# Filter spectra of an FFT layer stored with a frequency's 32 channels side by side, through three slots and copies on POOL

## The reference

```
qkv = x @ w_qkv;  q = softmax(q, -1);  k = softmax(k, tokens)      # 4 heads of 32
x = x + layernorm((v^T k applied to q) @ w_out + b_out)
def _stu(u, sigma, phi, Mu, Mpp, Mpm):                              # u: (b, t, d)
    U_plus  = irfft(rfft(phi) * rfft(u))[:, :t]                     # 16 filters
    U_minus = the same on u with alternating signs
    return einsum('btkd,k,kde->bte', U_plus,  sigma**.25, Mpp)
         + einsum('btkd,k,kde->bte', U_minus, sigma**.25, Mpm) + ar(Mu, u)
t = t + sum over 4 fractions of _stu on the first T // frac tokens, weighted by a one-hot choice
```

## Time and profile before

| | |
|---|---|
| median of 3 runs | 379.24 us (376.47 to 379.54) |
| profiled execution: time, span | 377.4 us, 374.0 us |
| mean granted TensorE clock | 0.989 of full speed |
| PE busy | 341.5 us (91%) |
| DVE busy | 228.9 us (61%) |
| ACT busy | 190.7 us (51%) |
| POOL busy | 35.5 us (9%), 38 instructions |

### The profile page before, as it was taken

The page is one execution under the profiler, slowest core; times in us unless marked ns, Lnnn a source line. Parts: engine busy times, 40 slices in busy tenths (PEclk is TensorE's granted clock), DMA queues, the critical chain, the costliest instruction groups (busy, mean ns, idle before and its releaser), DMA issues.

```text
span 374.0 us, 9464 instructions
## 1 busy us (share of the span) xinstructions
PE 341.5 (91%) x4044; PEld 228.4 (61%) x4044; DVE 228.9 (61%) x461; ACT 190.7 (51%) x415; POOL 35.5 (9%) x38
## 2 busy tenths in 40 slices
PE   7969999999998999998889999799998899999890
PEld 2545666566646899956556379257646554773790
DVE  5679768689848403156956764643446476245894
ACT  2988688988868300044862656530346215033460
POOL 4027512122210001000000000000000000000000
PEclk9999999999999999999999999999999899999997
DMA  8960000000070000020000000000000000000004
GB/s 232 127 197 1 2 4 2 2 4 2 3 169 3 4 4 2 4 59 2 0 2 2 0 3 0 4 0 2 2 0 2 0 3 0 2 2 1 0 2 115
DMA packets 7426, 8.95 MB, mean 24 GB/s; under 512 B 3840, under 2 KB 6544, under 8 KB 7056
## 3 DMA queue, kind: packets, MB, share of 16 engines
q1 hardware_dynamic: 5718, 7.28, 9.1%
q10 hardware_dynamic: 1664, 1.05, 0.9%
HBM read 5.70 MB, written 1.05 MB: 18 GB/s over the span
## 4 chain that ended last, share of the span: by engine, by line
PE 64%; DVE 14%; ACT 10%; issue 5%; DMA 4%; SPq 2%; DVEq 0%; ACTq 0%
PE bank L665 30%; PE bank L1098 6%; PE bank L277 5%; PE bank L271 4%; DMA arena<-in_w_spec 4%; PE bank L1025 4%; PE bank L1036 3%; PE bank L865 2%; PE bank L889 2%; ACT lnv L376 2%; SPq L561 1%; ACT rs L381 1%; DVE arena L1796 1%; PE bank L778 1%; PE bank L1155 1%
## 5 line engine op out<-in xcount | busy, mean ns | idle before, releaser
L370 ACT ACTIVATE sq<-bank 128x512 f32<-128x512 f32 x33 | 19.4, 591 | 64.1 <-PE bank L271 50.4
L665 PE MATMUL bank<-xn,sb_w_attn 128*128 128x512 f32 x64 | 34.5, 621 | 3.7 <-ACT attn_scratch L1233 1.9
L665 PE MATMUL bank<-sb_consts 128*128 128x512 f32 (+1 forms) x80 | 35.4, 553 | 0.0
L277 PE MATMUL bank<-sq,sb_consts 128*128 128x512 f32 x66 | 34.7, 611 | 0.5 <-ACT sq L370 0.2
L376 ACT ACTIVATE lnv<-bank 128x512 f32<-128x512 f32 x33 | 19.7, 596 | 30.2 <-PE bank L277 29.9
L1098 PEld LDWEIGHTS bank<-arena,sb_w_late 128*128 128x128 f32 x180 | 23.0, 190 | 10.9 <-DVE arena L1854 8.0
L665 PE MATMUL bank<-arena 64*32 64x256 f32 (+4 forms) x466 | 26.6, 381 | 2.5 <-ACT arena L1266 1.2
L1098 PE MATMUL bank<-arena,sb_w_late 128*128 128x128 f32 (+1 forms) x180 | 26.4, 283 | 1.5 <-DVE arena L1854 0.3
L611 POOL TENSOR_TENSOR attn_scratch<-attn_scratch 128x512 f32<-128x512 f32 x16 | 20.4, 1275 | 72.1 <-DVE attn_scratch L1567 72.1
L1036 PE MATMUL bank<-arena,sb_w_late 128*128 128x128 f32 x136 | 26.3, 277 | 0.0
L1025 PE MATMUL bank<-arena,sb_consts 128*128 128x128 f32 x136 | 26.1, 276 | 0.1
(11 more groups left out here) (208 smaller groups left out, 625.3 us busy)
## 6 DMA issues: line engine op xcount, KB each, us to landing
sb_w_late<-in_w_late SPq DMA_DIRECT2D x1, 1100.5 KB, 18.6
arena<-in_w_spec SPq DMA_DIRECT2D x4, 256.0 KB
arena<-arena SPq DMA_DIRECT2D x4, 256.0 KB, 4.1
arena<-fourier SPq DMA_DIRECT2D x1, 768.0 KB, 16.4
sb_w_attn<-in_w_attn SPq DMA_DIRECT2D x1, 641.0 KB, 8.2
xR<-in_x ACTq DMA_DIRECT2D x4, 128.0 KB, 3.1
xR<-in_x SPq DMA_DIRECT2D x4, 128.0 KB, 4.1
arena<-arena SPq DMA_DIRECT2D x4, 128.0 KB, 2.3
```

The costliest lines, as they stand in the source:

```text
L277: pe.matmul(bank[:, var_bank(i), :], mean32, sq[:, i % 2, :], start=True, stop=True)\
L370: act.activation(sq[:, i % 2, :], bank[:, centre_bank(i), :], ACT.Square).then_inc(S("ln_squared"), 1)
L665: return mm(ps, lhsT, rhs, start=True, stop=True)
```

## The change

FI becomes 1: w lies as (n e) for each part, a frequency's 32 channels side by side, and one channel's frequencies 32 floats (128 bytes) apart. ACT's second and third activation of a turn no longer write to `w_f`, but without gaps to `turned`, three slots (turn m uses m mod 3) that lie in the memory of `toep`. POOL copies a slot to `w_f` in `spread_turn(m)`, two copies a turn, 32 in all, each counting `spectra`. In POOL's stream the copies of a step's turns stand ahead of `q_normalise` of the same unit. New waits: POOL for `filt_sb` of the turn; ACT, from turn 3 on, ahead of its second activation for the copies of turn m - 3; SP ahead of the toep DMAs for all 32 copies; TensorE ahead of the first pass for all 32.

```diff
--- before.py
+++ after.py
@@ -56,7 +56,8 @@
 HT = T // 2
 FREQ = HT
 LAGS = T // 4
-FI = 8
+FI = 1
+TURNS = 3
 TRI_ORDER = [2, 3, 0, 1]
 DFT_BANKS = [6, 7, 0, 1, 2, 5, 3, 7]
 
@@ -171,6 +172,9 @@
         SEG_T = [None, None, T // 4, T // 8]
         SEG_AT = [None, None, 0, T // 4]
         toep = arena[:, AT_TOEP:AT_TOEP + N_TOEP].rearrange("p (t e) -> p t e", e=C)
+
+        turned = arena[:, AT_TOEP:AT_TOEP + 2 * TURNS * 4 * FREQ]\
+            .rearrange("p (w m k n) -> p w m k n", w=2, m=TURNS, k=2)
 
 
 
@@ -576,6 +580,7 @@
 
             sp.wait_ge(S("filt_zero"), 1)
             sp.wait_ge(S("filt_sb"), C // 2)
+            sp.wait_ge(S("spectra"), C)
             for n in (3, 2):
                 for r in range(NQ):
                     sp.dma_start(toep[C * r:C * r + C, SEG_AT[n]:SEG_AT[n] + SEG_T[n], :],
@@ -612,7 +617,17 @@
                 pool.sem_inc(S("q_norm"), 1)
 
 
+            def spread_turn(m):
+                pool.wait_ge(S("filt_sb"), m + 1)
+                for w_ in (1, 0):
+                    to = slice(0, 2 * C if w_ else P)
+                    pool.tensor_copy(w_f[w_][to, m::C // 2, :, :],
+                                     turned[to, w_, m % TURNS, :, :].rearrange("p k (n i) -> p k n i", i=FI))\
+                        .then_inc(S("spectra"), 1)
+
             for u in range(U):
+                for m in filter_turn(u, 0) + filter_turn(u, 1):
+                    spread_turn(m)
                 q_normalise(u)
                 if u == 0:
                     pool.wait_ge(S("sig4"), 1)
@@ -896,6 +911,7 @@
 
             pe.wait_ge(S("x_f_act"), 4)
             pe.wait_ge(S("x_f_dve"), 4)
+            pe.wait_ge(S("spectra"), C)
             frequencies(0, slice(0, P), w_fr[0])
             segment(2, 8, 16).then_inc(S("stu_ps"), 1)
 
@@ -1261,10 +1277,10 @@
                 act.wait_ge(S("filt_ps"), m + 1)
                 act.activation(filt[2 * C:, AR:, m::C // 2].rearrange("p t e -> p e t"),
                                bank[2 * C:, 4:6, 2 * FREQ:2 * FREQ + LAGS], ACT.Copy)
-                act.activation(w_f[1][0:2 * C, m::C // 2, :, :],
-                               bank[0:2 * C, 4:6, 2 * FREQ:4 * FREQ].rearrange("p k (n i) -> p k n i", i=FI), ACT.Copy)
-                act.activation(w_f[0][:, m::C // 2, :, :],
-                               bank[:, 4:6, 0:2 * FREQ].rearrange("p k (n i) -> p k n i", i=FI), ACT.Copy)\
+                if m >= TURNS:
+                    act.wait_ge(S("spectra"), 2 * (m - TURNS + 1))
+                act.activation(turned[0:2 * C, 1, m % TURNS, :, :], bank[0:2 * C, 4:6, 2 * FREQ:4 * FREQ], ACT.Copy)
+                act.activation(turned[:, 0, m % TURNS, :, :], bank[:, 4:6, 0:2 * FREQ], ACT.Copy)\
                     .then_inc(S("filt_sb"), 1)
 
             for i in range(U + 3):
```

## The result

The changed kernel takes 376.16 us (median of 20 runs, 373.50 to 378.73) against 379.04 (20 runs, 376.47 to 381.08): ratio 0.9926, 95% interval 0.9905 to 0.9946, so 2.9 us less. A repeat of 12 runs gave 0.9935 [0.991, 0.9959].

The account below looks back on a forecast made before the run. The prediction took TensorE to bound the kernel, with both frequency passes on the chain. Passes -7.4 us, ScalarE, DMAs and waits 0, POOL's lateness absorbed: 377.4 to 370.0 us, 371.8 against the median; range 368.5 to 380.0.

Parts of the forecast that it names:

- The moving read: TensorE's w read in both frequency passes: without the step, 30.6 ns a record falls to 16.4, a pass to 4.4 us.
- Rival B: In the passes: weight loads bind, not the w read; nothing gained, 379 us; chance 0.13.
- its soft form: In the passes: loads at 22.4 ns a record, only -4.3 us, 374.9 us; chance included in the forecast's 0.70.
- ScalarE, slots, waits: In attention: 32 activations write 512 contiguous floats instead of runs of 8, new waits already satisfied; 0 us.
- POOL: In attention: 32 copies at 1.27 us each fit beside the query sums; temporary lateness of 2 to 4 us goes again.
- the threshold of 1.4: POOL's budget in attention: copies under 1.4 us fit in 64.0 us; each 0.1 us more costs 3.2 us.
- Rival A: In attention: POOL's copies ahead of query sums become the bound, kernel ends slower, up to 388 us; chance 0.17.
- The bound of 1.9: Upper bound for a POOL copy of 512 elements, from line 619 at 3.4 ns an element: 1.9 us.
- Is all of it on the path?: Around both passes: work behind them has early inputs or hides DVE's transposes as before, so both cuts count in full.
- the 7.4: Forecast saving of the two frequency passes together: -7.4 us, between -8.9 and -4.3.
- The clock: TensorE's granted clock, read as 1.00, its upper level, in all the stretches.
- The sum against the median: Whole kernel: profiled 377.4 us, 1.8 below median 379.24, less 7.4 gives 370.0; against the median 371.8 us.

Follow-up runs that it names:

- e3_fi8_pool: Changed kernel with the old layout FI = 8, slots and POOL copies kept: 378.98 us, ratio 0.9998 to before.
- e2_shift_stream: Changed kernel with 16 small extra matmuls (64 instructions) at the end of attention, ahead of the passes: 372.67 us, one profiled run.
- e9_both_covered: Changed kernel with five segment(2) steps moved into pass one and two filler matmuls in pass two: 371.94 us, ratio 0.9827 to before.
- e11_before_covers: Kernel before (FI = 8) with five segment(2) steps moved into pass one and two fillers in pass two: 379.31 us, ratio 1.002 to before.
- e1_fill_pass2: Changed kernel with two filler matmuls of 512 columns in the middle of pass two: 371.97 us (4 runs), ratio 0.9809.
- e1b_fill_pass2: Changed kernel with two fillers in pass two, run again beside the changed kernel itself: 372.76 us (6 runs), ratio 0.9866.
- e10_fi2_both_covered: Kernel before with FI = 2 written directly by ScalarE, segment(2) steps in pass one, two fillers in pass two: 373.55 us, ratio 0.9846 to before.
- e14_one_filler: Changed kernel with five segment(2) steps in pass one and one filler matmul, not two, in pass two: 374.46 us, ratio 0.9899.
- e6_work_between: Changed kernel with five segment(2) steps moved into pass one and centre_tri(0) into pass two: 374.21 us, ratio 0.9891.
- e13_cover_pass1: Changed kernel with only five segment(2) steps moved into the middle of pass one: 373.59 us, ratio 0.9876.

## Why the prediction was wrong in size

**The moving read: right.** The step was the cost: 30.6 ns a record became 16.0, where 16.4 was taken from the load's mean of 140 ns as 0.33 of the way. The pass without its pause is 4.5 us, where 4.4 was forecast. Rival B (loads bind, nothing gained) is out, and so is its soft form: the load takes 147 ns, not 200. Why a record takes 16.0 and not the 13.5 of its columns no run tells, and that a third of the way between two load durations came out so near may be luck.

**ScalarE, slots, waits: right**, 0 us within 1.3 (0.579 us, `e3_fi8_pool` at 0.9998). Its own direct write costs 1.09 us, which is 0.5 us more for 512 elements, where line 1262's rows had 0.11 more for 128: scaled by four, 0.45.

**POOL: right in what followed, too dear in the price.** 1.27 us was taken, 1.10 measured in the mean; the threshold of 1.4 was not reached by any copy (1.24 the longest), and POOL waits for DVE. Rival A is out. The bound of 1.9 from line 619 was far off; whether that line's scalar column is the reason, as the prediction suspected, no run shows. The two figures that the prediction has beside its own, 769 ns without a step and the estimate of 1.24 us with it, lie above the 609 (in runs of 8) and 1.10 us measured.

**The step that failed** is "Is all of it on the path?" and its words "So both cuts count in full, and nothing else becomes late there." I asked that of every engine and every buffer but not of the supply of TensorE's own instructions. This supply was the next limit: 256 instructions last 2.05 us at the new pace, while packets start 3.5 us apart and their instructions run 2.3 to 2.9 us later. It gave back 1.0 us in pass one and 1.5 in pass two (`e2_shift_stream` and the 768 instructions show that it is this, `e9_both_covered` against `e11_before_covers` that the 7.4 come out whole once both passes are covered). No rival had it. The profile of before had the hint: in the passes the instruction packets start 3.7 to 4.2 us apart, closer than anywhere before them, and a record in half the time would ask for one every 2.05.

**The clock** was taken as 1.00 in all stretches and left so. A further 2.0 us went there, one low stretch more in the mean run. It is gone where both passes are covered (1.7 stretches); that a pause brings it, and how, is not shown beyond this association.

**The sum against the median:** the profiled run of before was 1.8 us below the median, and I added these 1.8 to both sides. The table says what they were: its clock was at the first step (0.989), and 37 of 62 runs lie at the second. The profiled run of the changed kernel was again on its kernel's own best step. Comparing two profiled runs gives 3.6 us, the medians 2.9; the same step gives the 5.0 that TensorE's work is worth.

## What to carry to other kernels

- Before counting a faster instruction in full, ask for how long 256 instructions of its engine last then. On TensorE here 3.9 us had no pause, and two blocks of 2.05 us in a row had one at their end. Break such a run in the middle with some 2 us of longer matmuls that are due anyway, and see first what they hide where they stand now.
- A moving read with floats 8 bytes apart costs what a gapless one does; 16 bytes apart it costs 1.9 times (64 columns, four column strips). A layout that interleaves two is often enough, and an ordinary ScalarE write makes it (609 against 579 ns).
- Sort the runs by their mean granted clock before explaining 1% effects; a profile shows one run at one step. What the change gains is still told by all runs, as it may move the clock too. And where two kernels differ by a change and by its side effect, put the same remedy on both: 2.9 us became 7.4.

## What the runs showed of the hardware that was not expected

- Instruction fetch binds TensorE: pauses of 0.6 to 1.8 us where 256 records of 16.0 ns and their loads follow each other, moved by exactly 32 records when 64 instructions stand ahead. Packets of 16 KB start 3.35 us apart or more around the passes, and their instructions run 2.3 us after the start at the earliest.
- Writes of single floats at a 128 byte step: 1.09 us for 128x512 on ScalarE (0.58 gapless or in runs of 4 and 8, 0.61 in runs of 2), 1.10 on POOL (0.61 in runs of 8).
- The low clock comes in portions of one size, 1.7 us of full clock lost over some 3.4 us, one to five in a run (the end from 365 us on left out); their number varies from run to run of one kernel.
- The time outside the span is 3.3 to 4.1 us in every kernel but those with added TensorE instructions (`e1_fill_pass2`, `e1b_fill_pass2`, `e2_shift_stream`, `e9_both_covered`, `e10_fi2_both_covered`, `e11_before_covers`, `e14_one_filler`), where it is 1.6 to 1.9, in all of their runs. Moving instructions without adding any (`e6_work_between`, `e13_cover_pass1`) doesn't bring it. It makes 1.8 of the 4.2 us by which `e9_both_covered` beats the changed kernel, and it is why the covers cost `e11_before_covers` only 0.4 us in all although its span is 2.3 longer. No run tells what it is.
